# A relational graph network on one core: the messages of a tile moved from behind the next tile's last sums to behind its second group of sums

## The reference

```
for l in range(4):
    h   = einsum('ni,rio->rno', X, weights[l])        # messages: 4 products of each node
    msg = h[etype, src] * inv_deg[:, None]            # one row of 256 for each edge
    agg = segment_sum(msg, dst)                       # summed at the destination
    out = agg + X @ roots[l] + biases[l]
    out = (out - mean(out)) * rsqrt(var(out) + 1e-5) * gammas[l] + betas[l]
    X   = elu(out) + X
```

## Time and profile before

| | before |
|---|---|
| median of 3 runs | 2629.09 us (2626.32 to 2634.03) |
| the profiled execution | 2628.71 us, its span 2626.9 us |
| granted clock of PE, mean | 0.805 |
| PE, DVE, POOL busy | 82%, 55%, 59% of the span |
| gathers | 1568, 0.961 us each |
| sums (halves) | 3712, 0.475 us each |

### The profile page before, as it was taken

How to read it: one execution, slowest core, us unless ns; L and a number is a source line. 1 busy time by engine, 2 the same in 40 slices (tenths; PEclk the granted TensorE clock), 3 DMA queues, 4 the chain that set the end, 5 groups by cost and what they waited for, 6 DMA issues and landing times.

```text
span 2626.9 us, 43114 instructions
## 1 busy us (share of the span) xinstructions
PE 2162.1 (82%) x7317; PEld 1284.5 (49%) x7320; DVE 1449.0 (55%) x4907; ACT 276.9 (11%) x538; POOL 1544.4 (59%) x1630
## 2 busy tenths in 40 slices
PE   4489667788888898888888989888889798887775
PEld 2254456664445554344455553445555444445554
DVE  6560999973445664234455652344556423456677
ACT  1114003310001111000011110000111100000000
POOL 3200600037777773777777737777777377777773
PEclk8589559996789998567889995678999956667778
DMA  5013300013444443334444433344444433334342
GB/s 165 0 41 144 130 8 0 0 42 106 120 129 138 145 149 96 105 105 121 129 136 146 145 104 104 106 120 129 138 145 147 140 110 104 105 104 121 105 121 64
DMA packets 103215, 280.43 MB, mean 107 GB/s; under 512 B 27676, under 2 KB 39050, under 8 KB 102798
## 3 DMA queue, kind: packets, MB, share of 16 engines
q0 software_dynamic: 75264, 205.62, 27.5%
q10 hardware_dynamic: 18224, 62.59, 6.2%
q1 hardware_dynamic: 9566, 10.42, 1.3%
HBM read 219.61 MB, written 58.91 MB: 106 GB/s over the span
## 4 chain that ended last, share of the span: by engine, by line
PE 50%; issue 13%; POOL 12%; DVE 9%; DMA 9%; DVEq 2%; POOLq 1%; ACT 1%; SPq 0%; ACTq 0%
PE acc L544 27%; POOL ring L335 12%; DMA ring<-h_rows,idx 8%; PE hp L463 8%; PE pw L463 7%; PE acc L533 3%; DVE S L993 3%; PE acc L536 2%; DVE hot_n L966 1%; DVE hot_s L966 1%; POOLq L204 1%; PE tr L452 1%; ACT XT L580 1%; DVEq L993 1%; PE pw L439 1%
## 5 line engine op out<-in xcount | busy, mean ns | idle before, releaser
L335 POOL DMA_INDIRECT ring<-h_rows,idx x1568 | 1506.3, 961 | 988.4 <-issue 715.2
L544 PE MATMUL acc<-ring,S 128*128 x3712 | 1247.8, 475 | 174.1 <-SPq L255 131.1
L1016 DVE TENSOR_SCALAR S<-iota,ecol 128x128 f32<-128x128 f32 x1856 | 611.7, 367 | 857.3 <-PE acc L544 753.8
L544 PEld LDWEIGHTS acc<-ring,S 128*128 128x128 f32 x3712 | 751.9, 224 | 662.0 <-issue 588.5
L463 PE MATMUL hp<-wts,XT 128*128 (+1 forms) x416 | 220.9, 681 | 22.4 <-ACT XT L580 22.4
L463 PE MATMUL pw<-wts,XT 128*128 (+1 forms) x384 | 197.9, 663 | 20.3 <-ACT XT L580 20.3
L533 PE MATMUL acc<-wts,XT 128*128 (+1 forms) x400 | 121.6, 432 | 62.3 <-issue 62.3
L966 DVE TENSOR_TENSOR hot_s<-iota,place 128x400 bf16<-128x400 f32 x196 | 111.5, 569 | 90.6 <-PE acc L494 85.8
L463 PEld LDWEIGHTS hp<-wts,XT 128*128 128x128 f32 x416 | 86.9, 220 | 126.2 <-issue 126.2
L533 PEld LDWEIGHTS acc<-wts,XT 128*128 128x128 f32 x400 | 81.0, 210 | 118.9 <-issue 110.0
L651 ACT ACTIVATE work<-work 128x256 f32<-128x256 f32 x100 | 41.7, 417 | 899.6 <-DVE work L1045 890.3
(11 more groups left out here) (243 smaller groups left out, 1085.6 us busy)
## 6 DMA issues: line engine op xcount, KB each, us to landing
h_rows<-hst ACTq DMA_DIRECT2D x100, 512.0 KB, 3.0
ring<-h_rows,idx POOLq DMA_INDIRECT x1568, 2.8
wts<-weights SPq DMA_DIRECT2D x32, 128.0 KB, 2.8
x_rows<-X ACTq DMA_DIRECT2D x1, 3200.0 KB, 10.0
wts<-x_rows ACTq DMA_DIRECT2D x1, 3200.0 KB, 11.5
X<-x SPq DMA_DIRECT2D x1, 3072.0 KB
out<-X ACTq DMA_DIRECT2D x2, 1024.0 KB
wts<-roots SPq DMA_DIRECT2D x8, 128.0 KB, 3.0
```

Source lines behind the costliest of these rows:

```text
L335: pool.indirect_dma_start(ring[:, k, :], None, h_gather, bass.IndirectOffsetOnAxis(ap=idx[:, g * J + j:g * J + j + 1], axis=0)).then_inc(l ...
L544: nc.tensor.matmul(accs[t % 2][:, 0:D], S[:, at * J + j, :], ring[:, bass.ds((c + j) % SLOTS, 1), :].rearrange("p a d -> p (a d)"), start= ...
L1016: v.tensor_scalar(S[:, at * J + j, :], iota[:, t * P:(t + 1) * P], dst_c[:, bass.ds(c + j, 1)], inv_c[:, bass.ds(c + j, 1)], ALU.is_equal, ...
```

## The change

`aggregate` takes a function, `between`, and calls it after its second group of sums, before the loop over the remaining groups. In layers 0 to 2 this function issues transposes and products of tile t-1. Nothing changes on DVE, ACT, POOL or SP, nor in layer 3, and tile 24's own messages stand where they stood.

```
-            def aggregate(l, t, lm, lg):
+            def aggregate(l, t, lm, lg, between=None):
 ...
                 for i in range(2):
                     four(lo_t + i * J, i)
+                if between is not None:
+                    between()
                 with pe.Fori(lo_t + 2 * J, end_t, J) as c:
                     four(c, 0)
 ...
             with pe.Fori(0, L - 1) as l:
+                def messages(t):
+
+                    e = l * NT + (t + NT)
+                    turn(e, t)
+                    node_products(e, t, l + 1, e if t == 0 else e - 1)
+
                 for t in range(NT):
-                    aggregate(l, t, lm, lg)
-                    if t > 0:
-                        e = l * NT + (t + NT - 1)
-                        turn(e, t - 1)
-                        node_products(e, t - 1, l + 1, e if t == 1 else e - 1)
+                    aggregate(l, t, lm, lg, (lambda t=t: messages(t - 1)) if t > 0 else None)
                 e = l * NT + (2 * NT - 1)
                 turn(e, NT - 1)
                 node_products(e, NT - 1, l + 1, e - 1)
```

## The result

The changed kernel takes 2713.6 us (median of 4 runs, 2710.9 to 2723.26), the kernel before 2630.03 (4 runs). The ratio is 1.0324, 95% interval 1.0294 to 1.0355: slower by 3.2%, where 2714 us was forecast. The profiled execution is the longest of the four, 2723.26 us with a span of 2721.4.

The account below looks back on a forecast made before the run. Gathers and PE alternate as the bound, both at their limit in tiles 11 to 23. Three layers of 27.5 us plus 2.9 once give 85.4, added to 2628.7 for 2714 us; own range 2680 to 2750, wider range 2654 to 2780.

Parts of the forecast that it names:

- The place: Tiles 11 to 23, where gathers and PE are both at their limit: 26.4 us of delay per layer, landing in POOL's gap.
- The mechanism: In tiles 11 to 23 PE reaches the transposes before DVE's normalized X and idles about 1.3 us each.
- R+6.44: X ready 6.44 us after R, the moment a tile's last sum is done, with statistics starting at R+1.6.
- The clock: PE's idle time brings 1.2 GHz stretches in the 13 tiles: 1.4 us per tile, making 14.2 instead of 12.8.
- the sign to look for: Granted clock in the stretch of tiles 11 to 23 falls from 0.99 to about 0.8.
- Rival B: The clock holds in tiles 11 to 23: 12.8 us per tile, 2656 us in all; chance 0.22.
- rival C: Each stall slows all the products, and loads or middle tiles add their gap: 15.7 us per tile, 2777 us; chance 0.16.
- Table loads on PE: Four table loads per tile, 2.6 us, hidden behind products and sums in tiles of 12 sums: costed at nothing.
- The step that failed: Tiles of 16 sums or more: loads' gap appears but costs nothing, PE's 15.3 us staying under 16.3 us of gathers.
- the upper bound of 3.08: On DVE, the latest start of the normalization's statistics, R+3.08, as before the change; 1.6 was taken.
- The term for the 13 tiles: Tiles 11 to 23 of each layer: 184.6 us against 158.2, 26.4 us of delay per layer.
- that for the layer ends: Uncovered last normalization adds 1.1 us per layer; last products at 1.2 GHz add 2.9 us once.

Follow-up runs that it names:

- the shorter normalization: Changed kernel with one Newton step instead of three in the normalization: 2644.19 us, ratio 1.0062 to the kernel before.
- The filled gap: Changed kernel with four matmuls nobody reads in PE's idle time in tiles 11 to 24, three ahead of the transposes, one ahead of the products: 2688.16 us, ratio 1.0237.

## Why the prediction was right

**The place.** It put the loss in the 13 tiles in which gathers and PE are level, and said that it would land in POOL's gaps. 86 of 94.6 us are in the gaps, the gathers are 1.259 us apart and don't pause, and with the old order from tile 11 on there is no loss at all.

**The mechanism.** It said that PE would come to the transposes before X, and wait 1.3 us. It waits 1.36 to 1.6 in the rows shown, and in every one of tiles 12 to 24, 76.5 us in 42 instances; without the three layer ends of 4.9 each that is 1.58 a tile. X was put at R+6.44 and is ready at R+6.66, with the statistics at R+1.79 instead of 1.6. That this wait is the cause, and not the order as such, is shown by the shorter normalization: the wait shrinks to 0.54 in the rows shown and 69 of 85 us go, 60 of them between tile 10 and tile 23.

**The clock.** Its sign was right and its size was not. It was priced at 1.4 us per tile on the average, 55 us in 39 tiles, from layer 3's granted clock of 0.82; the stretch has 0.94, and the sign to look for was "about 0.8". The filled gap puts its cost at 20 to 34 us. From tile 10's last sum to tile 23's the three layers take 187.9, 180.2 and 180.3 us, 14.45, 13.86 and 13.87 per tile, against the forecast's 14.2; before, it was 158.3, 158.0 and 158.7 in all. These averages come near 14.2 only because tile 11 takes 15.2 us for a reason that the sum had at nothing (next paragraphs) and because the wait is 1.58 and not 1.3. Rival B (12.8 per tile, 2656) was nearly the filled kernel's tile, rival C (15.7 each) no layer's.

**Table loads on PE.** Costed at nothing in tiles of 12 sums. In tiles 12 to 24 that holds, and there the root follows the last sum without a gap (1530.72); this agrees with the queue of 64 places that the prediction takes from the Trainium skill ("TensorE: Matmul & The Clock Gate", the table at its head). It does not hold in tile 11, which has 12 sums but follows a tile of 16: its root waits 1.95 to 1.99 us in each layer. It was said that the gap would appear from 16 sums on, and it does: 60 instances before the root instead of 30.

**The step that failed.** "In tiles of 16 sums or more ... it costs nothing" rested on 15.3 us per tile, 1.93+5.23+0.94+3.51+3.65. The terms measure 2.16+6.93+0.94+3.51+3.62 = 17.16 in tile 10 of layer 1, against 16.3 of gathers. What was mis-sized is the second one, root, bias and eight sums: behind 2 us of idle time part of them ran at 1.2 GHz, and the sum had no clock in these tiles. X is late there too, at R+8.1 to 8.4 and not R+6.5: DVE reads its tables after the last selections, which come late, and its statistics start at R+3.4, beyond the upper bound of 3.08. PE comes 0.7 us later still, so in the changed kernel its own work ends last, and DVE's takes over as soon as PE's loads are moved. Tile 10's last sum comes 5.3, 3.0 and 3.5 us late, which the sum had at zero; it is 12 us in all. The run with the new order from tile 11 on (73 of 85, with intervals that nearly meet) agrees, and so does the one with the table reads moved on both engines.

**How much of the hit is luck.** The term for the 13 tiles was too large by 6 us (73.4 measured, 79.2 forecast), with the clock in it too large by 21 to 35; that for the layer ends was nearly right (5.0 against 6.2: layer 1's end took 27.5 for 27.3); tiles 1 to 10 were missing with 12. The mechanism was forecast, but 2714 and 2713.6 agree that closely because errors cancel.

**What stays open.** 5.9 us of the profiled execution's excess lie in layer 3, whose instructions are the same. From its first gather to the end it takes 536.6 us, 530.7 before, and 529.5 to 535.7 in the profiles of the other runs with the same layer 3, so this is spread between executions and not the change. The other timed runs are 8 to 12 us shorter than the profiled one, and no profile tells where. Why layer 0 has more slow tiles (7 of 12) than layers 1 and 2 (5 each) is not known.

## What to carry to other kernels

A producer's work that waits for another engine should stand as far behind its input as the queue allows: count the time from the input's last contribution, on both engines, before moving it forward. Where an engine is level with a fixed-pace transfer, each microsecond of new wait per tile adds up and shows only at the next barrier; where it has room, the same wait costs nothing. Reads of loop bounds from memory are free only while their sequencer can run ahead, so count how many groups without a late dependency stand in front of them, and look at both engines: here moving them on PE alone gained nothing, since DVE's result came only 0.7 us ahead of PE.

## What the runs showed of the hardware

Idle time of 1.35 to 1.95 us on PE, then two transposes and 0.56 us more, was followed by products at part speed (5.24 to 6.69 us for 3.67) in 19 of 39 tiles of 12 sums; with 1.46 us of matmuls whose result nobody reads put there, and one more in the 0.56 us, in none; with a wait of 0.35 to 0.99 us (one Newton step), in none either. Idle time of 1.95 to 2.19 us before the root was followed by eight sums in 5.25 to 5.41 us instead of 3.72 in all of tiles 7 to 11 of the changed kernel's three layers; but with one Newton step tiles 8 and 10 of layer 2 had 2.0 us and then 3.72, so the length of the gap alone does not decide it. Table loads follow each other every 0.67 us on PE (four of them from 1529.0 to 1531.0), and three on DVE take about 2.2 us.
